# A four-layer network on one core: two joins between stages interleaved

## What is computed

```
h = layernorm(x) * (1 + c) + s
x = x + g * stage(h)          # c, s, g from silu(cond) @ wmod, one set per batch and stage
```

```
L0_ffn:   gate, up = h Wg, h Wu (256 -> 688);  out = (silu(gate) * up) Wd
L1_attn:  q, k, v = h Wq, h Wk, h Wv; 32 score maps of 8 features, causal softmax;
          a = softmax_even - lam * softmax_odd;  out = rmsnorm_per_head(a v) Wo
L1_ffn:   logits = h Wr (8 experts); the two largest, softmaxed, are the gates;
          out = sum_e gate_e * (h We_e + be_e)
```

## Time and profile before

| | |
|---|---|
| three runs | 2097.16, 2099.39, 2099.85; median 2099.39 |
| the profiled execution | 2101.8, of which the span in the trace is 2100.0 |
| TensorE busy | 1850.9, 88% of the span |
| VectorE busy | 1373.0, 65% |
| POOL, ScalarE busy | 895.8 (43%), 741.1 (35%) |
| mean granted TensorE clock | 0.936 of the full one |

### The profile page before, as it was taken

How to read it: one execution, slowest core, us unless ns; L and a number is a source line. 1 busy time by engine, 2 the same in 40 slices (tenths; PEclk the granted TensorE clock), 3 DMA queues, 4 the chain that set the end, 5 groups by cost and what they waited for, 6 DMA issues and landing times.

```text
span 2100.0 us, 40010 instructions
## 1 busy us (share of the span) xinstructions
PE 1850.9 (88%) x13400; PEld 1270.9 (61%) x13400; DVE 1373.0 (65%) x3587; ACT 741.1 (35%) x1511; POOL 895.8 (43%) x965
## 2 busy tenths in 40 slices
PE   8999999689995999999999968998967888998887
PEld 5555555489993455555555436676756666885443
DVE  4767677465552556565656537888845776886775
ACT  2544444112221465555555531111122223443332
POOL 0345454565653254545454332233333223663233
PEclk7999999799998999999999988999999888999887
DMA  6100000100003745454545300000011000000111
GB/s 230 52 9 5 7 5 9 31 9 8 10 10 68 158 87 106 89 103 90 100 89 103 68 11 9 9 7 7 10 33 43 15 13 17 14 16 13 35 37 40
DMA packets 68177, 93.34 MB, mean 44 GB/s; under 512 B 9852, under 2 KB 62316, under 8 KB 64748
## 3 DMA queue, kind: packets, MB, share of 16 engines
q1 hardware_dynamic: 68076, 92.01, 19.3%
HBM read 61.70 MB, written 29.49 MB: 43 GB/s over the span
## 4 chain that ended last, share of the span: by engine, by line
PE 68%; DVE 19%; issue 6%; POOL 2%; ACT 2%; DMA 2%; SPq 1%; DVEq 1%; POOLq 0%; ACTq 0%
PE PS L1020 16%; PE PS L1965 3%; PE PS L668 3%; PE PS L1841 3%; PE PS L725 3%; PE PS L1175 3%; DVE negmax L2185 2%; PE PS L741 2%; PE PS L507 2%; DVE xn L497 2%; PE PS L722 2%; PE PS L1893 2%; PE PS L1896 2%; PE PS L1945 1%; PE PS L1938 1%
## 5 line engine op out<-in xcount | busy, mean ns | idle before, releaser
L2185 DVE TENSOR_REDUCE negmax<-PS 128x2 f32<-128x512 f32 (+1 forms) x384 | 246.9, 684 | 211.2 <-PE PS L1885 106.0
L538 POOL TENSOR_TENSOR X<-X,y_sb 128x512 f32 (+1 forms) x128 | 165.2, 1291 | 150.1 <-DVE y_sb L533 145.1
L533 DVE TENSOR_TENSOR y_sb<-PS,ga_sb 128x512 f32<-128x512 f32 x96 | 66.2, 690 | 179.0 <-PE PS L769 50.1
L1020 PE MATMUL PS<-we_hi,h_parts 128*128 128x512 f32 x512 | 179.7, 412 | 0.0
L497 DVE TENSOR_SCALAR xn<-X,mv,rs 128x256 f32 (+1 forms) x256 | 155.3, 648 | 22.4 <-POOL rs L490 21.2
L517 ACT ACTIVATE hT<-PS,modT 128x256 f32<-128x256 f32 x256 | 130.0, 559 | 105.6 <-PE PS L507 104.6
L2104 ACT ACTIVATE pw<-PS 128x512 f32<-128x512 f32 x256 | 139.0, 600 | 75.2 <-PE PS L1941 75.2
L488 POOL TENSOR_TENSOR rs<-mv,eps 128x2 f32<-128x2 f32 x128 | 26.6, 208 | 296.3 <-DVE mv L481 296.1
L1020 PE MATMUL PS<-l_h_parts,lut_hi 128*128 128x256 f32 (+1 forms) x768 | 145.5, 291 | 6.7 <-POOL l_h_parts L1143 6.7
L1509 DVE SCALAR_TENSOR_TENSOR l_acc<-PS,rt_g,l_acc 128x256 f32<-128x256 f32 x256 | 106.1, 475 | 30.6 <-PE PS L1020 25.5
L1020 PEld LDWEIGHTS PS<-l_h_parts,lut_hi 128*128 128x128 f32 (+1 forms) x768 | 117.8, 184 | 9.6 <-issue 5.4
(11 more groups left out here) (270 smaller groups left out, 4383.2 us busy)
## 6 DMA issues: line engine op xcount, KB each, us to landing
ga_sb<-ga_dram SPq DMA_DIRECT2D x128, 128.0 KB, 2.9
qk_dram<-qk_parts SPq DMA_DIRECT2D x64, 192.0 KB, 2.8
KS<-qk_dram SPq DMA_DIRECT2D x32, 384.0 KB, 5.7
QS<-qk_dram SPq DMA_DIRECT2D x32, 384.0 KB, 9.5
qk_dram<-qk_parts SPq DMA_DIRECT2D x64, 128.0 KB, 2.8
wmod<-in_wmod SPq DMA_DIRECT2D x4, 1536.0 KB, 14.0
qk_dram<-qk_parts SPq DMA_DIRECT2D x64, 64.0 KB, 2.5
y_out<-X SPq DMA_DIRECT2D x16, 256.0 KB, 2.2
```

Of the source, the lines that this page charges most:

```text
L538: pool.tensor_tensor(xb(b), xb(b), y_sb[b.par][:, :, :], ALU.add).then_inc(s.x.sem, 1)
L1020: last_ = pe.matmul(out, x.bitcast(F32R), y.bitcast(F32R), start=start and n == 0, stop=stop and n == 2)
L2185: dve.tensor_reduce(to, src, AX.X, ALU.max, negate=True).then_inc(s.max.sem, 1)
```

## The change

**The first join** (L0_ffn to L1_attn). In slot 15 of the feed-forward, transpose and modulate of the attention's batch 0 come after tile m = 1 and not 2. TensorE then does the k projection of batch 0 after tile 2, q after tile 3, v and the transpose of batch 1 after tile 5, into banks 5, 6 and 7, which the feed-forward leaves free. ScalarE evicts k after its silu of tile 3, q after tile 4, v after tile 5, and modulates batch 1. VectorE applies the layernorm of batch 1 after tile 2. POOL splits k after its low part of tile 4 and q after that of tile 5. In the attention these steps are left out for batch 0, and the k and q projections of batch 1 move to the front of slot 0, before the first score pair.

**The second join** (L1_attn to L1_ffn). In slot 16 of the attention, VectorE starts with the weights' split, the high part of batch 0's h between its two operations, and the layernorm of batch 1; POOL does the low part of h; TensorE does units 0 and 1 around the last values of batch 15 and unit 2 behind out(14). Slot 17 is not run on TensorE, ScalarE and VectorE; what it held for batch 15 (normed_T, copy, out, norm, y) is handed over in `left` and stands in slot 0 of the expert stage, between batch 0's logits, units and accumulations. The waits of that stage for the last y and X are replaced by narrower ones. In memory QS and KS of one batch now lie side by side, and we_hi lies over those of the even batches, h_parts over the parts.

The diff, cut to its core (the helpers split out of loops are the code of before):

```diff
@@ the feed-forward, TensorE (l0f_tensor) @@
-                        if m == 2:
+                        if m == (1 if i.reg is None and i.off == B - 1 else 2):
                             ahead(ln_transpose, pe, pl, i, 1)
+                        if i.reg is None and i.off == B - 1:
+                            for n in {2: (0,), 3: (1,), 5: (2, 3)}.get(m, ()):
+                                l1a_first_projection(pe, sigs[pl + 1], n)
@@ ScalarE (l0f_scalar) @@
-                        if m == 2:
+                        if m == (1 if i.reg is None and i.off == B - 1 else 2):
                             ahead(modulate, act, pl, i, 1)
+                        if i.reg is None and i.off == B - 1 and m in (3, 4):
+                            l1a_first_eviction(act, sigs[pl + 1], m - 3)
+                    if i.reg is None and i.off == B - 1:
+                        l1a_first_eviction(act, sigs[pl + 1], 2)
+                        further(modulate, act, pl + 1, 1)
@@ VectorE and POOL (l0f_vector, l0f_pool) @@
+                        if m == 2 and i.reg is None and i.off == B - 1:
+                            further(ln_apply, dve, pl + 1, 1)
+                        if m >= 4 and i.reg is None and i.off == B - 1:
+                            l1a_split(pool, sigs[pl + 1], Idx(None, 0), 5 - m, 2 * m - 8)
@@ the attention, TensorE slot (l1a_tensor) @@
+                if pl and i.reg is None and i.off == 0:
+                    project_k(c)
+                    project_q(c)
                 if i.ok:
                     max_pair(i, 0, 0)
...
-                if c.ok:
+                if c.ok and not first_two(c):
                     project_k(c)
...
                 if i.ok:
                     max_pair(i, 2, 0)
+                tail(i, 0)
                 if d.ok:
                     values(d, 3)
+                tail(i, 1)
...
                 if e.ok:
                     out(e)
+                tail(i, 2)
...
+            def tail(i, n):
+                if pl + 1 < len(sigs) and i.reg is None and i.off == B:
+                    l1f_early(pe, pl + 1, sigs[pl + 1], n)
@@ the attention, VectorE slot, and POOL slot @@
+                if pl + 1 < len(sigs) and i.reg is None and i.off == B:
+                    l1f_weights(dve, pl + 1, sigs[pl + 1])
+                if pl + 1 < len(sigs) and i.reg is None and i.off == B:
+                    l1f_low_bits(pool, sigs[pl + 1], Idx(None, 0))
@@ new functions of the expert stage @@
+        def l1f_early(pe, pl, s, n):
+            if n == 0:
+                pe.wait_ge(*sigs[pl - 1].max(Idx(None, B - 1)))
+                pe.wait_ge(setup["we_lo"], 1)
+            l1f_unit(pe, s, Idx(None, 0), n)
+
+        def l1f_weights(dve, pl, s):
+            before = sigs[pl - 1]
+            dve.wait_ge(w_in[3], 16 * len(weights[3]))
+            dve.wait_ge(*before.score(Idx(None, B - 2)))
+            for b in (Idx(None, B - 2), Idx(None, B - 1)):
+                for c in range(2):
+                    dve.wait_ge(*scratch_ready(b, c))
+            split_hi(dve, we_hi[:, :, :, :], l1_we[:, :, :, :]).then_inc(setup["we_hi"], 1)
+            l1f_high_bits(dve, s, Idx(None, 0))
+            dve.wait_ge(setup["we_hi"], 1)
+            dve.tensor_tensor(we_lo[:, :, :, :].bitcast(F32R), l1_we[:, :, :, :], we_hi[:, :, :, :], ALU.subtract).then_inc(setup["we_lo"], 1)
+            further(ln_apply, dve, pl, 1)
@@ the expert stage, TensorE slot 0 (l1f_tensor) @@
+                if i.reg is None and i.off == 0:
+                    logits(pe, pl, s, b, l1_gw)
+                    pe.wait_ge(*before.y(last_b - 1))
+                    further(ln_transpose, pe, pl, 1)
+                    l1f_unit(pe, s, b, 3)
+                    gates_T(pe, pl, s, b, 6)
+                    bias(b)
+                    pe.wait_ge(*s.h(i + 1))
+                    normed_T()
+                    l1f_unit(pe, s, b, 4)
+                    out()
+                    l1f_unit(pe, s, b, 5)
+                    logits(pe, pl, s, i + 1, l1_gw)
+                    l1f_unit(pe, s, b, 6)
+                    l1f_unit(pe, s, b, 7)
@@ VectorE slot 0 (l1f_vector) @@
+                if i.reg is None and i.off == 0:
+                    route(dve, pl, s, b)
+                    norm()
+                    accumulate(b, 0)
+                    gate_out()
+                    accumulate(b, 1)
+                    ahead(ln_stats, dve, pl, i, 2)
+                    accumulate(b, 2)
+                    l1f_high_bits(dve, s, i + 1)
+                    route(dve, pl, s, i + 1)
+                    accumulate(b, 3)
+                    return
```

More of the change, by code:

```diff
@@ L429, in build @@
         work = ExitStack()
-        sb("beside", [P, 8 * 1024 // 4 + beyond // 4], F32, work)
+        sb("beside", [P, early_at // 4], F32, work)
         we_hi = sb("we_hi", [P, KH, E, D], F32, work)
+        sb("between", [P, (early_h - taken[work]) // 4], F32, work)
         h_parts = wbuf("h_parts", [P, 2, KH, T])
@@ L1418, in l1f_tensor, with bias @@
             pe.wait_ge(w_in[3], 16 * len(weights[3]))
-            pe.wait_ge(setup["we_lo"], 1)
+            pe.wait_ge(*before.u(last_b))
+            pe.wait_ge(*before.oT(last_b))
+            def bias(b):
+                pe.wait_ge(*s.gT(b))
+                if (b - 1).ok:
+                    pe.wait_ge(*s.acc0(b - 1))
+                for tt in range(TT):
+                    last_ = pe.matmul(bank(7)[:, tt * D:(tt + 1) * D], rt_gT[:, tt * P:(tt + 1) * P], l1_eb[:, :],
+                                      start=True, stop=True)
+                last_.then_inc(s.bias_ps.sem, 1)
@@ L1449, in slot @@
                             logits(pe, pl, s, i + 1, l1_gw)
-                else:
-                    ahead(ln_transpose, pe, pl, i, 1)
-                    if (i + 1).ok:
-                        logits(pe, pl, s, i + 1, l1_gw)
-            slots(pe, slot, -1, (4, 14), B - 1)
+            slots(pe, slot, 0, (4, 14), B - 1)
         def l1f_scalar(act, pl, s):
+            copy_ogT, = left[act.engine]
             memory_free(act, pl)
@@ L1467, in slot @@
                     act.activation(l1_acc[b.par][:, :, :].rearrange("p t d -> p (t d)"), bank(7), ACT.Copy).then_inc(s.acc0.sem, 1)
-                ahead(modulate, act, pl, i, 1)
+                if i.reg is None and i.off == 0:
+                    copy_ogT()
+                if i.reg is None and i.off == -1:
+                    further(modulate, act, pl, 1)
+                else:
+                    ahead(modulate, act, pl, i, 1)
                 if (i + 1).ok:
@@ new lines, in l1a_split @@
+        def l1a_split(pool, s, b, c, n):
+            hi, mid, lo = (qk_parts[b.par][:, a, c, :] for a in range(3))
+            pool.wait_ge(*(s.k if c else s.q)(b))
+            pool.tensor_tensor(qk_rest[:, c, :], qk32[:, c, :], hi, ALU.subtract).then_inc(s.split.sem, 1)
+            pool.wait_ge(*s.split(b, n + 1))
+            pool.tensor_tensor(mid, qk_rest[:, c, :], zero[:, :].broadcast_to([P, KH * T]), ALU.add).then_inc(s.split.sem, 1)
+            pool.wait_ge(*s.split(b, n + 2))
+            pool.tensor_tensor(lo, qk_rest[:, c, :], mid, ALU.subtract).then_inc(s.parts.sem, 1)
@@ L1830, in l1a_tensor @@
+        left = {}
         def l1a_tensor(pe, pl, s):
+            first_done = lambda c: pl > 0 and c.reg is None and c.off == 0
+            first_two = lambda c: pl > 0 and c.reg is None and c.off <= 1
             psum_free(pe, pl)
@@ L2057, in slot @@
                     max_pair(i, 2, 2)
-                if c.ok:
+                if c.ok and not first_done(c):
                     project_v(c)
@@ L2080, in slot @@
                     exp_pair(i, 1, 1)
-            slots(pe, slot, -2, LOOP2, B + 1)
+            def tail(i, n):
+                if pl + 1 < len(sigs) and i.reg is None and i.off == B:
+                    l1f_early(pe, pl + 1, sigs[pl + 1], n)
+            slots(pe, slot, -2, LOOP2, B if pl + 1 < len(sigs) else B + 1)
+            left[pe.engine] = (lambda: normed_T(Idx(None, B - 1)), lambda: out(Idx(None, B - 1)))
         def l1a_scalar(act, pl, s):
+            first_done = lambda c: pl > 0 and c.reg is None and c.off == 0
             memory_free(act, pl)
@@ L2158, in slot @@
                     exps(i, 1, 1)
-            slots(act, slot, -2, LOOP2, B + 1)
+            slots(act, slot, -2, LOOP2, B if pl + 1 < len(sigs) else B + 1)
+            left[act.engine] = (lambda: copy_ogT(Idx(None, B - 1)),)
         def l1a_vector(dve, pl, s):
@@ L2245, in slot @@
                     mean_square(d)
-            slots(dve, slot, -3, LOOP2, B + 1)
+            slots(dve, slot, -3, LOOP2, B if pl + 1 < len(sigs) else B + 1)
+            left[dve.engine] = (lambda: norm(Idx(None, B - 1)), lambda: gate_out(Idx(None, B - 1)))
         def l1a_pads(pool, n):
```

170 lines of the change are left out of this document (96 added, 74 removed).

## The result

The changed kernel takes **2068.31** in the median (2065.49 to 2068.81), the kernel before 2098.27 beside it: ratio 0.9855, interval 0.9843 to 0.9868. The forecast was 2067.4, with a range of 2058 to 2080.

What follows compares the result with a forecast made beforehand. TensorE carries 68% of the chain, so gains must come from its waits at two serial joins: 12.4 + 19.6 = 32.0 off 2101.8 gives 2069.8, less 2.4 for the median of the runs 2067.4; range 2058 to 2080.

Steps and rivals of the forecast that it cites:

- First join, the first pair: Feed-forward to attention: score pair 0 starts at 659.0, 10.2 earlier, as k and q are projected, split and written earlier.
- Slot 0: Attention's slot 0: k(1) and q(1) ahead of the first score pair give between 0 and 4.6, taken as 2.2.
- rival 4: First join: moved work does not matter, its wait returns at batch 1's load of QS; within 4 of before; chance 0.03.
- The hold of POOL: Second join: we_hi's cast gets between POOL's second and third small operation on the last maxima; everything behind 1.4 later.
- rival 1: Second join: POOL loses the port race twice, or units cost more at lower clock; gain 14 to 16, 2072; chance 0.13.
- The sign that I had named: Second join: the prediction is wrong if a split operation delays the maxima's parts by over 2.
- Units ahead of by_token: Second join: expert units 0 and 1 on TensorE ahead of by_token(15) make it and the root 1.5 later.
- Behind the root: Second join, root's end to gates_T(1): 18.2, the middle of 16.4 at the full clock and 20.0 at the lower.
- Second join: Attention to expert stage: gates_T(1) 19.6 earlier, middle of 21.4 at full and 17.8 at lower clock; ends 13.5 and 22.8.
- 2 (the DMA line dragged beside TensorE's work): First join: writes, loads or q split later, slot 0 gives nothing; 8 in place of 12.4, 2072; chance 0.13.
- 3 had the full clock in both places: Both joins at their upper end, above all the full clock: 14.8 + 22.8 = 37.6, 2062 or a little under; chance 0.10.
- 5 (slots with a slower rhythm): Attention: slots slower from their new start, maxima's load behind 12 writes; slower than before, over 2.3 per slot; chance 0.05.

Runs made afterwards that it cites:

- k1q1_in_slot0: The changed kernel with the k and q projections of batch 1 back between the score pairs of slot 0: 2069.77.
- units_later: The changed kernel with expert units 0 to 2 behind the first logits and the transpose of batch 1, not ahead of by_token(15): 2062.74.
- serial_handover: The changed kernel with batch 15's last steps ahead of the expert stage's logits, routing and accumulations on every engine: 2077.88.
- parts_first: The changed kernel with one more wait: VectorE starts the weights' split only when POOL has the last maxima's parts: 2064.59.
- all_four: The changed kernel with POOL's k/q splits one tile earlier, weights' split behind maxima's parts, units 0 to 2 behind logits, out(15) ahead of unit 4: 2057.85.
- all_five: all_four with VectorE's second quarter of accumulations ahead of batch 15's y: 2056.91.

## Why the prediction was right, step by step

- **First join, the first pair: 10.2 earlier; measured 11.1** (48.1 to 37.0 after y(13)), 11.4 by the means of the two traces of each kernel. The steps, with the 4.48 taken off by which y(13) itself came later: q split's end 642.9 forecast, 646.75 - 4.48 = 642.3 found; the sixth low half 639.4, found 638.8; the order k, low half, q as forecast. From the q split's end to the pair I had 16.1 and found 15.9. The idle of 4.64 is in the forecast's "under 6".
- **Slot 0: 2.2 of 0 to 4.6; measured 2.9** (2.4 by the means of two), and 3.2 by its own experiment. I chose the middle because the trace couldn't tell, so that it came close is partly luck. The price I had not seen is that batch 1's load waits in SP's queue behind the maxima's. In rival 4 I had let these loads land at 676.5, 11 before they were needed. SP issued them only at 678.10 and 679.03, behind the load of the maxima at 676.38, though the last writes had ended at 668.10, and 1.90 of wait appears as soon as k(1) and q(1) are later. In k1q1_in_slot0 the pair started 10.0 behind the end of these issues; by the same 10.0 the loads of the changed kernel landed near 690, for a pair at 690.98 (an estimate). The margin was about 1, not 11. The rival did not happen, but my argument against it was wrong.
- **Sum of the first join: 12.4; measured 13.8** by two traces of each kernel, 14.2 by all with the same code.
- **The hold of POOL: 1.4 later; measured 1.0** at the transpose and 0.7 behind it. It came in the place forecast, between the second and the third small operation. The Trainium skill (SBUF — State Buffer, section Who interferes with whom) says that whoever of the two starts first has the shared ports for the whole instruction. The third operation took 2.17, and the cast beside it had 2.1 to go; the one that adds epsilon took 4.43 beside we_lo's 4.46. Here the trace agrees, and the second hold of rival 1 did occur, on an operation that nobody was waiting for. So rival 1's mechanism was half right, and its second hold cost nothing. The sign that I had named, parts later by over 2, was missed narrowly: they were 2.0 later.
- **Units ahead of by_token: 1.5; measured 1.5** in units_later. The root's end 2.9 later than in the kernel before was forecast, 2.5 found between the two profiles.
- **Behind the root: 18.2** (16.4 at the full clock, 20.0 at the lower one, the middle taken); found **17.8**, with a clock of 0.54 for 7.5 of it. That the clock would be low for about half of the stretch was a choice of the middle, not a derivation, so the closeness of this term is partly luck. serial_handover shows that this was the part with the largest risk: with the same work and the lower clock all along, it takes 30.7.
- **Second join: 19.6; measured 20.5 against the profile I worked from, 19.9 against two, 18.4 by all with the same code.** The reference was itself 1.4 above the second execution up to gates_T(1), and 2.7 more behind it. I had taken off 2.4 for the whole execution, in the right direction.
- **Sum 32.0; medians 30.0, and 30.1 in a second set.** The joins gave 33.7 by two traces of each kernel and 32.6 by all. I had no term for the stretch ahead of them, which came 3 to 4 later with the changed code, and the kernel before stood at 2098.27 beside the result and not at 2099.39. That 2067.4 came within 1 of the result is partly luck; that the sum of the joins is within 2 of what was measured is not, as the steps inside them came where they were forecast.
- **Rivals.** 2 (the DMA line dragged beside TensorE's work) did not occur, writes took 8.10 as before. 3 had the full clock in both places; behind the root the clock was 0.54 for 7.5, and the joins' sum stayed under its 37.6. 5 (slots with a slower rhythm): slot 1 to the mean square of batch 14 took 517.1 before and 517.0 after.

What I missed altogether is that the change was not at its best: four of its choices cost 0.7 to 2.9 each, among them one that I had priced (the units ahead of by_token) without asking whether they had to stand there.

## What to carry to other kernels

When work is moved under a serial line of another engine, ask of each piece twice: does it stand in front of the line's start (then every microsecond of it moves the end), and does it keep TensorE busy until the line ends (then what followed ran at the full clock here)? Price a delay by the idle of the one who waits, not by the lateness of the one who releases. And measure a local change by distances between instructions around it, in more than one execution of the kernel before: here profiles of the same code differed by up to 3.4 in the very stretch that was changed.

## What the runs showed of the hardware

- A short POOL operation (128x32, 0.24 by itself) took 2.17 beside a cast of 4096 columns that started 0.21 ahead of it, and 4.43 beside a subtraction of 4096 columns; a VectorE product of 0.69 took 1.75 (at 1221.29) when a POOL subtraction of 1.26 had started 0.06 ahead. All three are from the trace of the changed kernel.
- POOL's long power operation behaves otherwise. In parts_first it started 0.16 behind the cast and took 7.58, which is its usual 5.44 and the 2.14 that the cast still had. From then on it ran its 5.44 beside the subtraction of 4096 columns, which took 4.41 and so was not held either:

```profile
1206.95 2.29 DVE L1023 CAST we_hi<-l_we 128x4096 fp32r<-128x4096 f32 x1 [0.82 <-POOL mparts L2433]
1209.56 4.41 DVE L1468 TENSOR_TENSOR we_lo<-l_we,we_hi 128x4096 fp32r<-128x4096 f32 x1
```

  It waited at its start and neither held nor was held afterwards; all_four and all_five show the same (7.57 and 7.58 beside a subtraction of 4.41). By the Trainium skill's rule (SBUF — State Buffer, section Who interferes with whom), as quoted above, it would have held the subtraction until 1214.7; the measurement decides.
- With the same work in the same join, TensorE's granted clock was 0.50 and then 0.64 over 31 in serial_handover, 0.54 over 7.5 in the changed kernel, and 1.00 all along in units_later (the windows are shown with the experiments). Ahead of those stretches TensorE had stood idle for 7.87 in the first, for 2.33, 0.46 and 0.79 in short turns in the second, and had been busy 12.5 of 14 in the third.
